# Output projection and the normalisation behind it as one stage for each small layer

## What is computed

```python
# layers 1 and 3
attn_out = attn @ out_w + out_b + residual
out = attn_out * rsqrt(mean(attn_out ** 2) + 1e-6) * postnorm_w
return gelu(out @ mlp_w1 + mlp_b1) @ mlp_w2 + mlp_b2 + residual
# layer 2
y = attn @ Wo + bo + hidden_state
return (y - mean(y)) * rsqrt(var(y) + 1e-6) * gamma + beta
```

## Time and profile before

| | |
|---|---|
| median of 3 runs | 1384.41 us (1384.3 to 1389.26) |
| the profiled execution: time, span | 1390.04 us, 1388.2 us |
| mean granted TensorE clock | 0.930 of full speed |
| busy share of the span | PE 89%, DVE 71%, ACT 52%, POOL 36% |
| layers 1 and 3, from the first transpose of `o` to the first MLP product | 25.75 and 25.79 us |
| layer 2, from the first transpose of `o` to the first transpose of layer 3 | 26.46 us |

### The profile page before, as it was taken

The page is one execution under the profiler, slowest core; times in us unless marked ns, Lnnn a source line. Parts: engine busy times, 40 slices in busy tenths (PEclk is TensorE's granted clock), DMA queues, the critical chain, the costliest instruction groups (busy, mean ns, idle before and its releaser), DMA issues. The chain is left out here.

```text
span 1388.2 us, 27413 instructions
## 1 busy us (share of the span) xinstructions
PE 1230.7 (89%) x9144; PEld 1014.5 (73%) x9144; DVE 987.8 (71%) x2229; ACT 722.0 (52%) x1636; POOL 495.6 (36%) x642
## 2 busy tenths in 40 slices
PE   5799999999599999999699699969499977699869
PEld 4699999999499999998588455559277756455558
DVE  6478878787578887888763689465488865689464
ACT  4456655666366666566542177441166632177441
POOL 3654545444374445543150000030199940000030
PEclk9899999999799999999899699979799998699979
DMA  4111111010211111010023874020660014874020
GB/s 151 47 31 32 31 30 30 23 30 1 95 32 32 31 31 29 9 38 0 31 65 71 121 83 56 13 77 1 196 131 3 2 51 83 112 81 55 13 65 31
DMA packets 55406, 70.90 MB, mean 51 GB/s; under 512 B 6696, under 2 KB 47404, under 8 KB 52976
## 3 DMA queue, kind: packets, MB, share of 16 engines
q1 hardware_dynamic: 53704, 65.83, 22.8%
q10 hardware_dynamic: 1600, 3.76, 0.9%
HBM read 46.79 MB, written 8.13 MB: 40 GB/s over the span
## 5 line engine op out<-in xcount | busy, mean ns | idle before, releaser
L945 ACT ACTIVATE a_prob<-a_s_ps,a_negmax 128x257 f32<-128x257 f32 x256 | 119.2, 477 | 92.9 <-DVE a_negmax L1027 92.9
L2033 DVE TENSOR_REDUCE s_mx<-s_s_ps 128x2 f32<-128x1024 f32 x128 | 151.9, 1211 | 17.9 <-PE s_s_ps L2078 17.6
L2018 ACT ACTIVATE s_probT<-s_st_ps 128x512 f32<-128x512 f32 x256 | 132.1, 605 | 58.6 <-PE s_st_ps L2092 56.3
L884 POOL TENSOR_TENSOR x_v_hi<-a_v_sum,x_one 128x512 fp32r<-128x512 f32 x60 | 63.2, 1053 | 248.7 <-DVE a_v_sum L1016 248.7
L1822 POOL TENSOR_SCALAR s_below<-s_masked,s_mx 128x256 f32<-128x256 f32 x256 | 117.8, 480 | 30.5 <-DVE s_mx L1850 29.7
L576 POOL TENSOR_TENSOR rstd<-base,power 128x4 f32<-128x4 f32 x4 | 4.0, 1009 | 335.6 <-DVE base L593 335.6
L1042 DVE TENSOR_TENSOR a_pT_lo<-a_t_ps,a_pT_hi 128x512 fp32r<-128x512 f32 x128 | 88.3, 690 | 37.9 <-ACT a_pT_hi L958 36.2
L1027 DVE TENSOR_REDUCE a_negmax<-a_s_ps 128x2 f32<-128x514 f32 x128 | 87.0, 689 | 35.6 <-PE a_s_ps L1088 35.3
L958 ACT ACTIVATE a_pT_hi<-a_t_ps 128x512 fp32r<-128x512 f32 x128 | 76.7, 600 | 59.5 <-PE a_t_ps L1142 56.1
L1850 DVE CUSTOM_DVE_ANT_0 s_masked<-s_s_ps,l_mask 128x256 f32<-128x256 f32 x256 | 90.7, 421 | 16.6 <-PE s_s_ps L1887 16.6
L1835 ACT ACTIVATE s_probT<-s_st_ps 128x512 f32<-128x512 f32 x128 | 69.9, 596 | 29.1 <-PE s_st_ps L1897 29.0
(11 more groups left out here) (289 smaller groups left out, 4069.0 us busy)
## 6 DMA issues: line engine op xcount, KB each, us to landing
a_wo_raw<-L_xattn_wo SPq DMA_DIRECT2D x16, 256.0 KB, 3.2
x_wqk_raw<-L_xattn_wq SPq DMA_DIRECT2D x31, 128.0 KB, 2.3
x_wqk_raw<-L_xattn_wk SPq DMA_DIRECT2D x31, 128.0 KB, 2.3
x_wv_raw<-L_xattn_wv SPq DMA_DIRECT2D x15, 256.0 KB, 3.0
l_k_st<-k_second SPq DMA_DIRECT2D x12, 256.0 KB, 9.6
l_k_st<-k_stack SPq DMA_DIRECT2D x16, 192.0 KB
l_q_st<-q_stack SPq DMA_DIRECT2D x12, 192.0 KB
x_vbias<-L_xattn_bias_v SPq DMA_DIRECT2D x2, 1024.0 KB, 11.0
```

The lines of the kernel that those rows point to most:

```text
L945: nc.scalar.activation(prob[:, n % 2, qt, 0:NK], s_ps[:, n % 2, qt, 0:NK], ACT.Exp, bias=negmax[:, n % 2, qt:qt + 1], accum_out=den[:, n % ...
L2018: nc.scalar.activation(probT[:, third % 2, n // 4, n // 2 % 2, n % 2], st_ps[:, u % 3], ACT.Exp, scale=c.scale).then_inc(z.exp_done, 1)
L2033: nc.vector.tensor_reduce(mx[:, i % 2, qt, a::2], s_ps[:, n % 2], AX.X, ALU.max).then_inc(z.max_done, 1)
```

## The change

`project_out` and `rms_turn` become `project_and_rms` (layers 1 and 3), `project_out` and `final_norm` become `project_and_scale` (layer 2). The output weights and the bias row get buffers that live through the attention, and SP loads them there: in round 11 of `pair_attention`, and in `wide_attention` behind its other loads. DVE copies two of the four turned groups, and ACT two. POOL adds the bias row (in layers 1 and 3 once all transposes are through, since the sum is written over `o_all`; in layer 2 at once). DVE adds a tile's product and takes that tile's statistics right behind it; half 0 has its `base` before the products of half 1 are added. DVE normalises tiles 6 and 7 alone and ACT the others. POOL makes `w1_lo` of one half between the two powers. In layer 2, ACT normalises tiles 0 to 5 after splitting the next weights. The transposes of the normalised tiles and their `hi` and `lo` parts are as before. The diff, cut to its core; the removed functions are those printed above:

```diff
-def rms_turn(core, name, src, ahead, eps, scale):
...
-def norm_and_mlp(core, layer, src, w1, b1, w2, b2, gelu, next_layer=None, out=None, scale=None, offset=None):
+def norm_and_mlp(core, layer, front, w1, b1, w2, b2, gelu, next_layer=None, out=None, scale=None, offset=None):
...
-            rms_turn(core, f"r{layer}", src, w, EPS, scale)
+            c, o_all, weights, dst = front
+            project_and_rms(core, f"r{layer}", c, o_all, weights, dst, w, EPS, scale)
...
@@ wide_attention, queue of SP
                 for b in range(1, B):
                     load_keys(c, sp, k_stack, k_st, b, batch_in[b])
                     load_queries(c, sp, q_stack, q_st, b, slice(0, NQ), batch_in[b])
+                weights.load(sp, z.out_in)
+                sp.wait_ge(z.out_in, 32)
@@ pair_attention, queue of SP
                     if first is not None and 7 <= first <= 10:
                         sp.wait_ge(z.st_done, NE * B)
                         late.load_head(c, sp, 3, first - 7, *slots[0], unit_in[2])
+                    if first == 11:
+                        weights.load(sp, z.out_in)
                 rounds(body)
+                sp.wait_ge(z.out_in, 32)
-def project_out(core, name, c, o_all, wo, bo, dst, next_layer=None):
...
-def final_norm(core, name, gamma, beta):
...
+class OutWeights:
+    def __init__(self, st, core, wo, bo):
+        self.core, self.wo, self.bo = core, core.ins[wo], core.ins[bo]
+        self.w, self.row = st.sb("w_out", [P, KT, D]), st.sb("b_out", [P, D])
+    def load(self, eng, sem):
+        eng.dma_start(self.w[:], self.wo.rearrange("(t p) n -> p t n", p=P)).then_inc(sem, 16)
+        eng.dma_start(self.row[:], self.bo.rearrange("(o n) -> o n", o=1).broadcast_to([P, D])).then_inc(sem, 16)
+class ProjectOut:
...
+    def turn(self, pe):
...
+    def place(self, kt, half):
+        return self.oT[:, kt, half * 512:(half + 1) * 512], self.t_ps[:, KT * half + kt]
+    def copy_vector(self, dve, half):
+        out, ps = self.place(0, half)
+        dve.wait_ge(self.z.turned, KT * half + 1)
+        self.nc.vector.tensor_copy(out, ps).then_inc(self.z.copied_dve, 1)
+    def copy_scalar(self, act, half):
+        out, ps = self.place(1, half)
+        act.wait_ge(self.z.turned, KT * half + 2)
+        self.nc.scalar.activation(out, ps, ACT.Copy).then_inc(self.z.copied_act, 1)
+    def add_bias(self, pool, in_place):
+        if not in_place:
+            pool.wait_ge(self.z.turned, 2 * KT)
+        for t in range(TT):
+            self.nc.gpsimd.tensor_tensor(self.dst[:, t], self.core.x[:, t], self.weights.row[:], ALU.add
+                                         ).then_inc(self.z.x_ready, 1)
+    def product(self, pe, t):
+        if t % 4 == 0:
+            pe.wait_ge(self.z.copied_dve, t // 4 + 1)
+            pe.wait_ge(self.z.copied_act, t // 4 + 1)
+        wait(pe, self.z.y_out, t - 3)
+        for kt in range(KT):
+            mm = self.nc.tensor.matmul(self.y_ps[:, t % 4, 0:D], self.oT[:, kt, t * P:(t + 1) * P],
+                                       self.weights.w[:, kt], start=(kt == 0), stop=(kt == KT - 1))
+        mm.then_inc(self.z.y_done, 1)
+    def add(self, dve, t):
+        dve.wait_ge(self.z.y_done, t + 1)
+        dve.wait_ge(self.z.x_ready, t + 1)
+        self.nc.vector.tensor_tensor(self.dst[:, t], self.y_ps[:, t % 4, 0:D], self.dst[:, t], ALU.add
+                                     ).then_inc(self.z.y_out, 1)
+    def observe(self, dve, t):
+        dve.wait_ge(self.z.y_out, t + 1)
+        observe(self.core, dve, self.dst, t, self.z)
+    def moments(self, dve, half):
+        for n in range(TT // 2):
+            t = half * TT // 2 + n
+            dve.wait_ge(self.z.stats_done, t + 1)
+            self.nc.vector.bn_aggr(self.core.mv[:, t, :], self.core.stats[:, t, :]).then_inc(self.z.mv_done, 1)
+        dve.wait_ge(self.z.mv_done, TT // 2 * (half + 1))
+def project_and_rms(core, name, c, o_all, weights, dst, ahead, eps, scale):
+    nc, HT = core.nc, TT // 2
     with core.stage(name) as st:
...
         with nc.Block() as block:
+            @block.sync
+            def _(sp):
+                ahead.prepare_sync(sp, z)
             @block.gpsimd
             def _(pool):
                 core.clear_used(pool)
+                out.add_bias(pool, False)
+                for half in range(2):
+                    deviation(core, pool, half, z, half)
+                    pool.wait_ge(z.hi_split, half + 1)
+                    nc.gpsimd.tensor_tensor(ahead.w1_lo[:, half], ahead.w1_raw[:, half],
+                                            ahead.w1_hi[:, half].bitcast(F32), ALU.subtract)
+            @block.tensor
+            def _(pe):
+                out.turn(pe)
+                for t in range(TT):
+                    out.product(pe, t)
+                for half in range(2):
+                    pe.wait_ge(z.normed_act, (4, 6)[half])
+                    if half:
+                        pe.wait_ge(z.normed_dve, 2)
...
             @block.scalar
             def _(act):
+                def high(n):
...
+                def normalise(t):
+                    act.wait_ge(z.rstd_done, t // HT + 1)
+                    nc.scalar.activation(normed[:, t], dst[:, t], ACT.Copy, scale=rstd[:, t:t + 1]
+                                         ).then_inc(z.normed_act, 1)
                 for half in range(2):
+                    out.copy_scalar(act, half)
+                ahead.prepare_scalar(act, z)
+                for t in range(4):
+                    normalise(t)
+                for n in range(2):
+                    high(n)
+                for t in range(4, 6):
+                    normalise(t)
+                for n in range(2, 4):
+                    high(n)
             @block.vector
             def _(dve):
+                def variance_and_square(half):
+                    out.moments(dve, half)
+                    mean, var = half_of(mv, half)[:, :, 0], half_of(mv, half)[:, :, 1]
+                    nc.vector.tensor_tensor(half_of(msq, half), mean, mean, ALU.mult).then_inc(z.msq_done, 1)
+                    dve.wait_ge(z.msq_done, half + 1)
+                    nc.vector.scalar_tensor_tensor(out=half_of(base, half), in0=half_of(msq, half), scalar=eps,
+                                                   in1=var, op0=ALU.add, op1=ALU.add).then_inc(z.base_done, 1)
+                def low(n):
...
                 for half in range(2):
+                    out.copy_vector(dve, half)
+                for half in range(2):
+                    for t in range(half * HT, (half + 1) * HT):
+                        out.add(dve, t)
+                        out.observe(dve, t)
+                    variance_and_square(half)
+                dve.wait_ge(z.rstd_done, 2)
+                for t in range(6, TT):
+                    nc.vector.tensor_scalar(normed[:, t, :], dst[:, t, :], rstd[:, t:t + 1], None, ALU.mult
+                                            ).then_inc(z.normed_dve, 1)
+                for n in range(4):
+                    low(n)
+def project_and_scale(core, name, c, o_all, weights, gamma, beta, next_layer):
+    nc, ins, x = core.nc, core.ins, core.x
+    HT = TT // 2
     with core.stage(name) as st:
...
         with nc.Block() as block:
             @block.sync
             def _(sp):
                 for row, src in ((g_row, gamma), (b_row, beta)):
                     sp.dma_start(row[:], ins[src].rearrange("(o n) -> o n", o=1).broadcast_to([P, D])
+                                 ).then_inc(z.rows_in, 16)
+                core.load_projections(sp, next_layer, z.next_in)
             @block.gpsimd
             def _(pool):
                 core.clear_used(pool)
+                out.add_bias(pool, True)
+                parts = list(core.weight_parts())
+                def split_low(n):
+                    raw, hi, lo = parts[n]
+                    pool.wait_ge(z.next_hi, n + 1)
+                    nc.gpsimd.tensor_tensor(lo, raw, hi.bitcast(F32), ALU.subtract)
+                deviation(core, pool, 0, z, 0)
+                split_low(0)
+                deviation(core, pool, 1, z, 1)
+                split_low(1)
+                split_low(2)
+            @block.tensor
+            def _(pe):
+                out.turn(pe)
+                for t in range(TT):
+                    out.product(pe, t)
+            @block.scalar
+            def _(act):
+                def normalise(t):
+                    act.wait_ge(z.shift_done, t // HT + 1)
+                    nc.scalar.activation(x[:, t], x[:, t], ACT.Identity, bias=shift[:, t:t + 1],
+                                         scale=rstd[:, t:t + 1]).then_inc(z.x_norm, 1)
+                for half in range(2):
+                    out.copy_scalar(act, half)
+                core.split_high(act, z.next_in, z.next_hi)
+                for t in range(6):
+                    normalise(t)
             @block.vector
             def _(dve):
+                def base_of(half):
```

(39 more changed lines are left out.)

205 lines of the change are left out of this document (51 added, 154 removed).

## The result

The changed kernel takes 1364.9 us (median of 4 runs, 1360.8 to 1369.8) where the kernel before took 1384.4 in the same comparison (4 runs, 1379.6 to 1389.3): a ratio of 0.986, 95% interval 0.983 to 0.989. That is 19.5 us less (by the interval 15 to 24); 17.9 was predicted.

A forecast was written before the change was run, and what follows sets the result against it. PE bounds the whole span, but the chain through DVE was taken to bound the three changed stages (78.0 us). Savings of 5.6 + 5.6 + 6.65 = 17.9 us from the 1384.4 median gave 1366.5, range 1359 to 1377.

The forecast's parts named there:

- Products: Merged stages: product 0 at 2.0 us behind the first transpose without DMA wait; in layers 1 and 3 instead of 2.67.
- Statistics and biases: Layers 1 and 3: statistics 0.35 us a tile behind each add; POOL's biases 0.74 each, ready ahead of the products.
- statistics are held too: Rival: DVE's statistics also wait for POOL in all three stages; 10.0 us less gained, 1376.5; chance 0.15.
- First base: Layers 1 and 3: ready at 8.4 us, including 1.1 for `msq` and `base` waiting on POOL's bias adds (ends 0 and 1.5).
- Second power: Layers 1 and 3: starts at 12.4 us behind the first transpose, over at 13.4.
- the tail: Layers 1 and 3: from DVE's last normalisation to the MLP, unchanged at 3.84 us, ending the stage at 20.1.
- Layer 2: Its merged stage: beta additions meet POOL's two `lo` parts, ending about 15.1; stage 19.8 instead of 26.5, 6.65 us less.
- Without any hold it would be 17.2: Layer 2: the stage's end in us if no DVE instruction waited for POOL, against 19.8 forecast.
- The load in the attention: Two DMAs per layer moved into the attentions: taken as 0 us; other end one row wait per layer, 5.9.
- the two cases with a row delayed: Pair attentions: one row per layer, 11.8 us back, 1378.4, chance 0.07; or repeated row waits, 1396.0, chance 0.04.
- first product still waits: Merged stages: the moved load fails to remove the product's wait; costs 3.1 us, 1369.6; no separate chance given.
- the 8.8 us of the rival: Clock recovers sooner at late transposes and MLP starts, holds on `msq` and `base` absent: 8.8 more gained, 1357.7; chance 0.11.

The follow-up runs named there:

- late load: Changed kernel with the loads of output weights and bias row moved back to the head of the merged stage: 1374.3 us (one run).
- both orders: Changed kernel; second `w1_lo` waits for DVE's two normalisations; in layer 2 one `lo` part precedes the second power, one enters the next projections: 1357.4 us, ratio 0.982.
- early load: Kernel before, old stages kept, with only the loads of output weights and bias row moved into the attention: 1382.3 us, ratio 0.997.
- idle turns: Changed kernel with PE transposing the identity, results unused, 26 times behind the last product and 12 behind the normalised tiles, layers 1 and 3: 1363.0 us.
- both `w1_lo` behind: Changed kernel with both `w1_lo` parts made by POOL after the second power, as in the old stage: 1365.7 us (one run).

## Why the prediction was right

The time, the sign and the mechanism were right; the stages save 2.6 us more than the 17.9 summed. What is off is the size of one term, the holds on the first base.

- **Products.** Forecast at 2.0 without a wait, came at 1.84. Add 0 at 3.0 (3.1), tiles 0.86 apart as forecast, then 0.79 (0.81).
- **Statistics and biases.** A `bn_stats` costs 0.43 beside any POOL work: the rival "statistics are held too" falls, and with it its 1376.5. POOL's biases took 0.69 each and never held an add back.
- **First base.** This term was mis-sized, as the range allowed: I charged 1.1 us for holds on `msq` and `base` and it was 0.44 (`msq` free, `base` held). The base was there at 7.6 instead of 8.4. Two thirds of the error in each of these layers is here, the rest in the earlier start.
- **Second power** at 11.5, not 12.4, for that reason. Behind it all came as forecast: one normalisation held for 2.4 (2.69 for two), the tail 3.9 (3.84), the clock's pattern kept. The end is 19.1 instead of 20.1. There was luck in it: the sum has no term for a hold on the second `msq`, which came just behind the first `w_w_lo` here and cost 1.65 us more where it came during it.
- **Layer 2.** The three additions of beta met POOL's two `lo` parts as forecast and ended at 14.9 (15.1); the stage ends at 19.2 (19.8). There is no term for a hold on `shift` either; it was free in this profile and costs 0.7 to 0.95 where POOL comes first. Two statements beside the sum were wrong. "Without any hold it would be 17.2": by the sum's own terms the additions would end at 13.4 instead of 15.1, and the stage at 18.1. And `base` is not safe for having one tensor input: with the late load one took 0.61 beside a bias, and in "both orders" one took 0.72 beside a `lo` part, where it takes 0.17 alone. In the changed kernel no POOL work stood beside it.
- **The load in the attention** was put at 0 with 5.9 as the other end. It cost nothing that shows: the waits for rows are unchanged (12.7 and 12.8), and the two cases with a row delayed fall. What I had wrong is the rival "first product still waits", priced at 3.1: that is the worth of the early load in the old stage (2.85 measured). In the merged stage it is worth 8.4 to 11.5, because the bias row too is waited for and DVE has nothing else to do, and in layer 2 also because the weights come late and the products then start at a slower clock (4.8 of the 8.4 is layer 2's). Had that rival come true, the time would have been 1375 to 1378 and not 1369.6 (1366.5 and the 8.4 to 11.5).
- **The clock.** The MLP's start was kept at 5.65 us at 0.50, and that was so; the idle turns show that the 8.8 us of the rival (less the holds' 2.2) was a fair price: 6.4 of 6.6 against the changed kernel's profile, 5.1 against the mean of the MLPs without idle turns.

## What to carry to other kernels

Price a load that is moved ahead in the stage as it will be, not as it is: what hides it may be the very work that the change takes away. Where DVE and POOL both have work at the end of a stage, put POOL's long instruction ahead of DVE's chain or behind it, by a wait if need be; one held DVE instruction costs up to the length of the POOL instruction, even when DVE's is of 128x4 elements. And look for the stretches in which PE waits for a few microseconds ahead of dense work: ahead of the two MLPs some two dozen transposes of nothing (13 and 12) cost nothing that shows and gave back about 2 us each, while 58 of them ahead of layer 3's projections gave back nothing that could be measured.

## What the runs showed that I had not expected

- A DVE instruction of 128x4 elements with two SBUF inputs takes 0.16 us alone and took 0.60, 1.09 and 1.81 beside POOL, and one with a single tensor input took 0.61 and 0.72 instead of 0.17. In "both `w1_lo` behind" it was the first `msq`, held 0.81 by a bias.
- The order of two engines at such a meeting changed between two executions of the same kernel and moved a stage by 0.95 us.
- A small load of a broadcast row took 3.2 us from issue to use in layer 1, and 4.7 with two larger loads issued behind it: here a transfer was delayed by what was issued after it.
- PE kept the full clock over an idle time of 1.93 us ahead of the last transposes in "both orders" and had lost it after 3.80 us in the changed kernel; behind those transposes it idled 2.03 us in "both orders" and opened the MLP at the slower level all the same. Idle times of 2.05 and 2.10 us in layer 2 ended at different levels. The length of the last idle time alone doesn't say which level follows.
